# One core of a post-norm decoder layer: new orders for the attention bodies, both LayerNorms applied by ScalarE in the next body

## What is computed

```python
def _layernorm(x, eps=1e-05):
    m = mean(x); v = var(x)
    return (x - m) / sqrt(v + eps)

def attn(x):          # 3 heads of width 512; the softmax runs over the query axis (axis=2)
    Q, K, V = einsum('bne,hde->hbnd', x, Wq), ..., ...
    w = softmax(einsum('hbnd,hbmd->hbnm', Q, K) / sqrt(512), axis=2)
    return mean(einsum('hbnm,hbmd->hbnd', w, V), axis=0) @ fc_w.T + fc_b

def xattn(q, latent): # 16 heads of width 32, keys and values from a 128-wide context, causal
    ...
    return softmax(where(causal, qh @ kh.T / sqrt(32), min)) @ vh @ Wout.T

def ffn(x):           # 64 experts, top 6 of a softmax router, capacity 128, plus one shared expert
    ...

x = _layernorm(x + attn(x))
x = _layernorm(x + xattn(x, ctx_512))
x = _layernorm(x + ffn(x))
```

## Time and profile before

| | before |
|---|---|
| median of 3 runs | 2343.31 us (2339.98 to 2346.21) |
| the profiled execution | 2345.75 us, span 2344.0 us |
| busy share of the span | TensorE 88%, VectorE 75%, ScalarE 42%, GpSimd 33% |
| one turn of the loop | 82.0 us, 14 turns |

### The profile page before, as it was taken

How to read it: one execution, slowest core, us unless ns; L and a number is a source line. 1 busy time by engine, 2 the same in 40 slices (tenths; PEclk the granted TensorE clock), 3 DMA queues, 4 the chain that set the end, 5 groups by cost and what they waited for, 6 DMA issues and landing times. The chain is left out here.

```text
span 2344.0 us, 50221 instructions
## 1 busy us (share of the span) xinstructions
PE 2062.7 (88%) x17648; PEld 1307.3 (56%) x17648; DVE 1759.2 (75%) x3790; ACT 980.6 (42%) x1515; POOL 772.8 (33%) x631
## 2 busy tenths in 40 slices
PE   7989899899889989989998953699999999999960
PEld 3556565566556556655655632466666666666640
DVE  5458888888788888878888877467777677776758
ACT  4324443443344344334433423355455554555533
POOL 1002412431342243134124314344444444454420
PEclk9999999999999999999999975799999999999985
DMA  6821001001100100110010041578788887877846
GB/s 215 110 110 40 11 29 38 18 20 38 38 9 29 38 19 19 38 38 9 29 38 12 17 142 52 149 238 247 228 251 238 244 247 229 250 238 245 247 131 243
DMA packets 132885, 268.71 MB, mean 115 GB/s; under 512 B 32304, under 2 KB 42544, under 8 KB 132848
## 3 DMA queue, kind: packets, MB, share of 16 engines
q1 hardware_dynamic: 108176, 226.13, 30.2%
q0 software_dynamic: 20480, 33.71, 7.2%
q10 hardware_dynamic: 4192, 8.39, 0.9%
HBM read 217.12 MB, written 51.12 MB: 114 GB/s over the span
## 5 line engine op out<-in xcount | busy, mean ns | idle before, releaser
L677 POOL TENSOR_SCALAR_AFFINE_SELECT x_plus_shared<-x_plus_shared 128x1024 f32<-128x1024 f32 x64 | 82.6, 1291 | 840.3 <-ACT x_plus_shared L889 840.1
L702 PE MATMUL ring<-xT_split,tion_then_expert_weights 128*128 128x256 f16 x2304 | 269.0, 274 | 7.5 <-POOL xT_split L655 3.8
L702 PE MATMUL ring<-tion_then_expert_weights,xT_split 128*128 128x512 f16 x1152 | 273.4, 390 | 1.4 <-issue 1.3
L873 ACT ACTIVATE x_plus_shared<-ring 128x512 f16<-128x512 f32 x224 | 130.2, 595 | 341.9 <-PE ring L702 309.0
L107 POOL DMA_INDIRECT slot_table<-table_records,slot_of_choice x192 | 228.3, 1189 | 86.0 <-issue 54.9
L702 PEld LDWEIGHTS ring<-xT_split,tion_then_expert_weights 128*128 128x128 f16 x2304 | 221.5, 98 | 45.0 <-issue 16.3
L702 PEld LDWEIGHTS ring<-tion_then_expert_weights,xT_split 128*128 128x128 f16 x1152 | 112.7, 100 | 138.8 <-issue 18.9
L991 DVE CUSTOM_DVE_ANT_0 quad<-quad,causal_penalty 128x128 f32<-128x128 f32 (+1 forms) x512 | 164.7, 394 | 30.7 <-PE quad L772 28.5
L1232 POOL DMA_INDIRECT expert_sums<-tion_then_expert_weights,scatter_index x64 | 151.4, 2365 | 59.0 <-POOL scatter_index L1229 55.7
L1007 DVE RECIPROCAL inv_denominator<-ring 128x256 f32<-128x256 f32 x64 | 111.9, 1749 | 68.7 <-PE ring L702 58.1
L953 DVE SCALAR_TENSOR_TENSOR x_plus_shared<-ring,x_plus_shared 128x512 f16<-128x512 f32 x192 | 130.3, 685 | 26.9 <-ACT x_plus_shared L873 26.3
(11 more groups left out here) (198 smaller groups left out, 4195.8 us busy)
## 6 DMA issues: line engine op xcount, KB each, us to landing
tion_then_expert_weights<-in_w_gate SPq DMA_DIRECT2D x64, 704.0 KB
tion_then_expert_weights<-in_w_up SPq DMA_DIRECT2D x64, 704.0 KB
tion_then_expert_weights<-in_w_down SPq DMA_DIRECT2D x64, 512.0 KB, 3.9
tion_then_expert_weights<-in_w_down SPq DMA_DIRECT2D x64, 192.0 KB, 4.0
xT_in<-in_xT SPq DMA_DIRECT2D x16, 512.0 KB, 4.4
x_in<-in_x SPq DMA_DIRECT2D x16, 512.0 KB, 3.4
expert_sums<-zero_rows SPq DMA_DIRECT2D x16, 512.0 KB, 12.9
x_rows<-x_plus_shared SPq DMA_DIRECT2D x16, 512.0 KB, 2.8
```

The costliest lines, as they stand in the source:

```text
L677: pool.affine_select(out=p32[:, g % 2, :, 0:2 * P], in_=p32[:, g % 2, :, 0:2 * P], compare_op=ALU.is_ge, fill=0.0, base=0, pattern=[[0, 4] ...
L702: last = pe.matmul(out_, left(a, c), right(b, c), start=(n == 0), stop=(n == 3 * chunks - 1))
L873: act.activation(half(0), src, ACT.Copy, scale=scale).then_inc(high, 1)
```

## The change

1. New orders of the steps for all four engines. In `PE_BODY` Y01 goes ahead of T, S00 and S01 ahead of M, V20 and V21 go behind S20, S21 and ST3. In `POOL_BODY` XB goes from the end to the place behind XS at the front, so that it waits for the O1 step of the body before; MASK2 goes ahead of the first group of scatters; the second and third group both stand behind MASK3, one right after the other, at the end of the list. In `DVE_BODY` AV1 goes behind the two last V steps, OUT0 ahead of O1.
2. VectorE's LN computes statistics, the inverse root and one new tile `shift` = -mean * rstd; it no longer applies the norms. The application goes to ScalarE as x * rstd + shift (ACTIVATE Identity), in the next body: NX2 (x2) behind Y00 and V00, NX1 (x1) behind TX.
3. VectorE's O0 now waits until ScalarE has done NX1 of this body, and OUT0 until NX2.

```diff
@@ -367,36 +367,37 @@
 
 
 PE_BODY = [
-    ("Y", 0, 0), ("C", 0, 0), ("V", 0, 0), ("V", 0, 1), ("TX", 0, 0), ("TX", 1, 0), ("T", 0, 0), ("T", 1, 0),
-    ("K", 0, 0), ("R", 0, 0), ("K", 1, 0), ("Q", 0, 0), ("Q", 1, 0), ("Y", 0, 1), ("M", 0, 0), ("C", 1, 0),
-    ("V", 1, 0), ("M", 1, 0), ("S", 0, 0), ("S", 0, 1), ("M", 2, 0), ("Y", 1, 0), ("M", 3, 0), ("Y", 1, 1),
-    ("V", 1, 1), ("MT", 0, 0), ("MT", 1, 0), ("S", 1, 0), ("ST", 0, 0), ("S", 1, 1), ("CT", 0, 0),
-    ("Y", 2, 0), ("ST", 1, 0), ("Y", 2, 1), ("ST", 2, 0), ("AV", 0, 0), ("V", 2, 0), ("S", 2, 0), ("S", 2, 1),
-    ("ST", 3, 0), ("AV", 1, 0), ("V", 2, 1), ("AV", 2, 0), ("O", 0, 0), ("AV", 3, 0), ("O", 1, 0),
-    ("OUT", 0, 0), ("OUT", 1, 0),
+    ("Y", 0, 0), ("C", 0, 0), ("V", 0, 0), ("V", 0, 1), ("TX", 0, 0), ("TX", 1, 0), ("Y", 0, 1), ("T", 0, 0),
+    ("T", 1, 0), ("C", 1, 0), ("K", 0, 0), ("R", 0, 0), ("Q", 0, 0), ("K", 1, 0), ("Q", 1, 0), ("S", 0, 0),
+    ("S", 0, 1), ("M", 0, 0), ("Y", 1, 0), ("M", 1, 0), ("V", 1, 0), ("M", 2, 0), ("Y", 1, 1), ("M", 3, 0),
+    ("V", 1, 1), ("MT", 0, 0), ("MT", 1, 0), ("CT", 0, 0), ("ST", 0, 0), ("S", 1, 0), ("S", 1, 1),
+    ("Y", 2, 0), ("ST", 1, 0), ("Y", 2, 1), ("ST", 2, 0), ("AV", 0, 0), ("S", 2, 0), ("S", 2, 1),
+    ("ST", 3, 0), ("V", 2, 0), ("V", 2, 1), ("AV", 1, 0), ("AV", 2, 0), ("O", 0, 0), ("AV", 3, 0),
+    ("O", 1, 0), ("OUT", 0, 0), ("OUT", 1, 0),
 ]
 ACT_BODY = [
-    ("C", 0, 0), ("V", 0, 0), ("Y", 0, 0), ("V", 0, 1), ("TX", 0, 0), ("TX", 1, 0), ("T", 0, 0), ("T", 1, 0),
-    ("K", 0, 0), ("K", 1, 0), ("Q", 0, 0), ("Q", 1, 0), ("Y", 0, 1), ("C", 1, 0), ("V", 1, 0), ("RM", 0, 0),
-    ("Y", 1, 0), ("S", 0, 0), ("S", 0, 1), ("Y", 1, 1), ("S1", 0, 0), ("V", 1, 1), ("ST", 0, 0), ("S", 1, 0),
-    ("S", 1, 1), ("P", 0, 0), ("Y", 2, 0), ("ST", 1, 0), ("S1", 1, 0), ("Y", 2, 1), ("P", 1, 0), ("ST", 2, 0),
-    ("V", 2, 0), ("P", 2, 0), ("S", 2, 0), ("S", 2, 1), ("ST", 3, 0), ("OM", 0, 0), ("S1", 2, 0), ("V", 2, 1),
-    ("P", 3, 0), ("OM", 1, 0), ("OM", 2, 0), ("OM", 3, 0),
+    ("C", 0, 0), ("Y", 0, 0), ("V", 0, 0), ("NX2", 0, 0), ("V", 0, 1), ("TX", 0, 0), ("TX", 1, 0),
+    ("NX1", 0, 0), ("Y", 0, 1), ("T", 0, 0), ("T", 1, 0), ("C", 1, 0), ("K", 0, 0), ("Q", 0, 0), ("Q", 1, 0),
+    ("K", 1, 0), ("S", 0, 0), ("Y", 1, 0), ("S", 0, 1), ("V", 1, 0), ("RM", 0, 0), ("Y", 1, 1), ("V", 1, 1),
+    ("S1", 0, 0), ("ST", 0, 0), ("P", 0, 0), ("S", 1, 0), ("S", 1, 1), ("ST", 1, 0), ("Y", 2, 0),
+    ("S1", 1, 0), ("Y", 2, 1), ("ST", 2, 0), ("P", 1, 0), ("P", 2, 0), ("S", 2, 0), ("OM", 0, 0), ("S", 2, 1),
+    ("S1", 2, 0), ("V", 2, 0), ("ST", 3, 0), ("V", 2, 1), ("P", 3, 0), ("OM", 1, 0), ("OM", 2, 0),
+    ("OM", 3, 0),
 ]
 DVE_BODY = [
-    ("Y", 0, 0), ("C", 0, 0), ("V", 0, 0), ("V", 0, 1), ("TX", 0, 0), ("TX", 1, 0), ("T", 0, 0), ("T", 1, 0),
-    ("K", 0, 0), ("R", 0, 0), ("K", 1, 0), ("RC", 0, 0), ("Q", 0, 0), ("Q", 1, 0), ("M", 0, 0), ("Y", 0, 1),
-    ("C", 1, 0), ("M", 1, 0), ("V", 1, 0), ("M", 2, 0), ("S", 0, 0), ("S", 0, 1), ("Y", 1, 0), ("S1", 0, 0),
-    ("M", 3, 0), ("Y", 1, 1), ("S2", 0, 0), ("MT", 0, 0), ("MT", 1, 0), ("V", 1, 1), ("RM", 0, 0),
-    ("S", 1, 0), ("S", 1, 1), ("CT", 0, 0), ("S1", 1, 0), ("RS", 0, 0), ("P", 0, 0), ("Y", 2, 0),
-    ("S2", 1, 0), ("Y", 2, 1), ("AV", 0, 0), ("P", 1, 0), ("V", 2, 0), ("S", 2, 0), ("S", 2, 1), ("P", 2, 0),
-    ("S1", 2, 0), ("AV", 1, 0), ("S2", 2, 0), ("V", 2, 1), ("OM", 0, 0), ("P", 3, 0), ("AV", 2, 0),
-    ("OM", 1, 0), ("AV", 3, 0), ("OM", 2, 0), ("OM", 3, 0), ("O", 0, 0), ("O", 1, 0), ("OUT", 0, 0),
+    ("C", 0, 0), ("Y", 0, 0), ("V", 0, 0), ("TX", 0, 0), ("TX", 1, 0), ("V", 0, 1), ("Y", 0, 1), ("T", 0, 0),
+    ("T", 1, 0), ("C", 1, 0), ("R", 0, 0), ("K", 0, 0), ("Q", 0, 0), ("RC", 0, 0), ("Q", 1, 0), ("K", 1, 0),
+    ("S", 0, 0), ("M", 0, 0), ("S", 0, 1), ("M", 1, 0), ("S1", 0, 0), ("Y", 1, 0), ("M", 2, 0), ("V", 1, 0),
+    ("M", 3, 0), ("Y", 1, 1), ("MT", 0, 0), ("MT", 1, 0), ("V", 1, 1), ("S2", 0, 0), ("RM", 0, 0),
+    ("S", 1, 0), ("CT", 0, 0), ("S", 1, 1), ("P", 0, 0), ("S1", 1, 0), ("RS", 0, 0), ("Y", 2, 0), ("Y", 2, 1),
+    ("S2", 1, 0), ("AV", 0, 0), ("S", 2, 0), ("S", 2, 1), ("P", 1, 0), ("S1", 2, 0), ("OM", 0, 0),
+    ("P", 2, 0), ("S2", 2, 0), ("V", 2, 0), ("V", 2, 1), ("AV", 1, 0), ("P", 3, 0), ("AV", 2, 0),
+    ("OM", 1, 0), ("AV", 3, 0), ("OM", 2, 0), ("OM", 3, 0), ("O", 0, 0), ("OUT", 0, 0), ("O", 1, 0),
     ("OUT", 1, 0), ("LN", 0, 0),
 ]
 POOL_BODY = [
-    ("XS", 0, 0), ("CS", 0, 0), ("MASK", 0, 0), ("MASK", 1, 0), ("SC", 1, 0), ("MASK", 2, 0), ("SC", 2, 0),
-    ("MASK", 3, 0), ("SC", 3, 0), ("XB", 0, 0),
+    ("XS", 0, 0), ("XB", 0, 0), ("CS", 0, 0), ("MASK", 0, 0), ("MASK", 1, 0), ("MASK", 2, 0), ("SC", 1, 0),
+    ("MASK", 3, 0), ("SC", 2, 0), ("SC", 3, 0),
 ]
 A_STEPS = {"Y", "V", "S", "S1", "S2", "O", "XS", "XB"}
 C_STEPS = {"NX2", "TX", "R", "RC", "RM", "CT", "RS", "SC"}
@@ -432,6 +433,7 @@
     stats = mem.sb("stats", [P, 2 * NB, 6], F32)
     mv = mem.sb("mean_var", [P, 2 * NB, 2], F32)
     rstd = mem.sb("rstd", [P, 2 * NB], F32)
+    shift = mem.sb("shift", [P, 2 * NB], F32)
     root_tmp = mem.sb("root_tmp", [P, 3, 2 * NB], F32)
     x1 = mem.sb("x1", [P, NB, E], F32)
     x1s = mem.sb("x1T_split", [P, 2, EC, N], F16)
@@ -499,6 +501,7 @@
     rmax, rexp = mem.sem("router_max"), mem.sem("router_exp")
     chosen_ready = mem.sem("chosen_ready")
     rec_used = mem.sem("records_used")
+    scaled = mem.sem("attention_row_scales")
     dve_step = mem.sem("dve_step")
     taken = mem.sem("waits_taken")
 
@@ -865,7 +868,20 @@
             def emit(b):
                 for s in b.act:
                     name, g, h = s
-                    if s in b.split:
+                    if name == "NX1":
+                        act.wait_ge(scaled, b.i)
+                        for t in range(NB):
+                            last = act.activation(x1[:, t, :], pre[:, t, :], ACT.Identity,
+                                                  scale=rstd[:, t:t + 1], bias=shift[:, t:t + 1])
+                        last.then_inc(ln1, 1)
+                    elif name == "NX2":
+                        act.wait_ge(scaled, b.i)
+                        act.wait_ge(x2_stored, b.n(0, 0, 16, 1))
+                        for t in range(NB):
+                            last = act.activation(x2[:, t, :], pre2[:, t, :], ACT.Identity,
+                                                  scale=rstd[:, NB + t:NB + t + 1], bias=shift[:, NB + t:NB + t + 1])
+                        last.then_inc(ln2, 1)
+                    elif s in b.split:
                         act.wait_ge(full, b.job(*s))
                         if name == "TX" and g == 0:
                             act.wait_ge(x2T_stored, b.n(0, 0, 16, 1))
@@ -921,22 +937,19 @@
                     links[0] += 1
                     dve.wait_ge(dve_step, done_before(b.i, LINKS_A, LINKS_B, LINKS_C) + b.i * LINKS_LN + (1 + links[0]))
 
-                def norm(parts):
-
-                    rows = [(at + t, pre[:, t, :], dst[:, t, :]) for at, pre, dst, _ in parts for t in range(NB)]
-                    for n, src, _ in rows:
+                def row_scales(rows):
+
+                    for n, src in rows:
                         last = dve.bn_stats(stats[:, n, :], src)
                     link(last)
                     own_wait(dve, taken)
-                    for n, _, _ in rows:
+                    for n, _ in rows:
                         last = dve.bn_aggr(mv[:, n, :], stats[:, n, :])
                     link(last)
                     n0, n1 = rows[0][0], rows[-1][0] + 1
                     inverse_root(dve, link, rstd[:, n0:n1], mv[:, n0:n1, 1], root_tmp[:, :, n0:n1])
-                    for n, src, dst in rows:
-                        last = dve.tensor_scalar(dst, src, mv[:, n, 0:1], rstd[:, n:n + 1], ALU.subtract, ALU.mult)
-                        if n % NB == NB - 1:
-                            last.then_inc(parts[(n - n0) // NB][3], 1)
+                    dve.scalar_tensor_tensor(shift[:, n0:n1], mv[:, n0:n1, 0], -1.0, rstd[:, n0:n1],
+                                             ALU.mult, ALU.mult).then_inc(scaled, 1)
 
                 for s in b.dve:
                     name, g, h = s
@@ -971,18 +984,19 @@
                         dve.wait_ge(full, b.job(*s))
                         if g == 0:
                             dve.wait_ge(xb_ready, b.n(1, 0, 0, 1))
+                            if b.b:
+                                dve.wait_ge(ln1, b.n(0, 1, 0, 1))
                         dve.scalar_tensor_tensor(pre[:, g, :], o[:, :], 1.0 / H, xb[:, g, :],
                                                  ALU.mult, ALU.add).then_inc(free, 1)
                     elif name == "LN":
-                        parts = []
+                        rows = []
                         if b.a:
                             dve.wait_ge(free, b.freed("O", 1, 0))
-                            parts.append((0, pre, x1, ln1))
```

(8 more changed lines are left out.)

## The result

| | median, us | range, runs |
|---|---|---|
| before | 2341.64 | 2337.86 to 2346.21, 4 |
| after | 2275.11 | 2274.09 to 2278.03, 4 |

The ratio is 0.9725, 95% interval 0.9708 to 0.9741. The changed kernel is 2.8% faster. The forecast was 2355, slower by 0.5%, with 2268 to 2385 as the range of 8 in 10; the measured time is that of rival B, 2275.

What follows compares the result with a forecast made beforehand. TensorE and VectorE, neither full, wait for each other in turn within a loop turn of 82.0 us. The new turn was 81.1 + 1.7 = 82.8, +11 us over 14 turns, making 2355 us; range of 8 in 10: 2268 to 2385.

Steps and rivals of the forecast that it cites:

- rival B: Behind AV3: nothing is held, GpSimd's chain bounds a turn of 76.2 to 77.1 us; time 2275, chance 0.25.
- LN: VectorE's LayerNorm application moved to ScalarE: TX's wait of 0.54 us goes, a gain of 0 to 0.6 per turn.
- M steps: TensorE's M steps, with Y01, S00 and S01 ahead: 1.5 us more waiting per turn, between 0 and 2.
- AV0's division: VectorE divides at once behind AV0, near 50.4 in place of 54.2 us; AV1's 2.53 wait and 1.7 of clock go.
- MASK3: GpSimd's step ahead of the eight scatters: ends near 59.8 us into the turn, where it ended at 62.9.
- the eight scatters: On GpSimd behind MASK3, without a break from 60.0 to 70.7 us, with 0.8 of stretch, between 0 and 1.5.
- The hold behind AV3: AV3's end, inside the scatter run, reaches VectorE 0.8 us after the run, at 71.5 not 66.5: 5.0, bounds 0 to 5.8.
- collision: VectorE's OM2 meets GpSimd's XS instead of OM1 meeting XB, before OUT0; costs 1.2 us in place of 3.45.
- the clock: TensorE behind a 6.8 us gap before OUT0: the 1.2 GHz level costs 1.7 us per turn, between 0 and 3.4.
- The landing: GpSimd waits for the last scatter to land before XS: 1.1 us, bounded by 0 and 2.
- CS: GpSimd's step behind XB, wanted by C0: done about 83.5 against 83.7 us, costing nothing, at most 0.5.
- A: The forecast itself: the hold moves from AV0 to AV3, -1.0 to +3.0 us per turn, 2330 to 2385; chance 0.57.

Runs made afterwards that it cites:

- e4: Changed kernel's four orders, with both LayerNorms still applied by VectorE as before the change; ratio to before 0.9724, turn 77.05 us.
- e6: Kernel before without the twelve scatters of each body; one run, only the turn is read: 78.33 us.
- e7: Changed kernel without the twelve scatters of each body; one run, only the turn is read: 74.00 us.
- e11: Kernel before with each scatter replaced by a GpSimd selection of about its length, each waited for; one run, turn 80.67 us.
- e14: e13 with GpSimd waiting for the landing after each fourth scatter; ratio to before 0.9861, turn 78.47 us.
- e15: e13 with GpSimd waiting for the landing after every scatter; ratio to before 0.9938, turn 78.42 us.
- e17: Kernel before, orders and places unchanged, with GpSimd waiting for the landing after each four scatters; ratio 1.0047, turn 80.96 us.
- e18: e8 with GpSimd waiting for the landing after each four scatters; ratio to before 0.9944, turn 79.39 us.
- e19: The changed kernel measured once more beside the kernel before; 2278.65 against 2354.82 us, ratio 0.9673, turn 77.08 us.
- e1: Kernel before with only MASK2 moved ahead of the first four scatters and MASK3 ahead of the last eight; ratio 1.0173, turn 84.35 us.
- e13: Kernel before with the twelve scatters moved into GpSimd's idle stretch of the next body; ratio 1.0250, turn 85.30 us.
- e12: Changed kernel with the scatters moved into the next body, behind XS, CS and XB; ratio to before 0.9608, turn 73.95 us.
- e16: e12 with the twelve scatters ahead of XB on GpSimd; ratio to before 0.9625, turn 73.89 us.
- e10: Changed kernel with MASK3 ahead of all twelve scatters, which then run in one row; ratio to before 1.0314, turn 86.76 us.
- e8: Changed kernel with CS ahead of XB at the front of GpSimd's body; ratio to before 0.9664, turn 75.82 us.

## Why the prediction was wrong

The unit, the two causes and most steps held. Times from Y00's first matmul, 668.00 in the shown turn, with the forecast in brackets:

- LN. TX's wait went, as predicted. e4 shows that this is worth nothing once GpSimd bounds the turn.
- M steps: 0.4 more, not 1.5. AV0 started at 48.8 (48.6), with the 0.83 of waiting for CS in it. The forecast's own parts, 48.1 - 0.54 + 1.5, give 49.1 and not 48.6, a slip of 0.5.
- AV0's division at 50.2 (50.4), no wait at AV1, no slow clock, no wait at O0 (0.4). MASK3 ends at 60.3 (59.8), the eight scatters at 71.3 (70.7), one of them stretched by 0.87 (0.8).
- **The hold behind AV3, the step that failed.** I took 5.0 us of VectorE's time, from 66.5 to 71.5, 0.8 us behind the end of the run. VectorE was free at 66.5 and divided at 67.25, in the middle of the run: it lost 0.75. OUT0 started at 70.5, not 75.9.
- Two further terms hung on it. OM2 and OM3 were done at 70.4, before XS began at 73.2: no collision (1.2). TensorE's largest gap was 1.15, and the clock stayed at 1.00 (1.7). The turn was 82.8 - 76.5 = 6.3 shorter than forecast: 5.4 for OUT0 and 1.7 for the clock, less 0.65 of waiting at Y00 and 0.15 for OUT itself.
- The landing took 1.94, not 1.1, within its bounds. CS was 0.83 late where I had taken nothing and at most 0.5.

The one long turn comes nearest to the forecast: VectorE idled 3.57 us behind AV3, OUT0 waited 3.97, and the granted clock was 0.68 over OUT0 and OUT1 (970.75 to 976.09). So what A expected of all turns happened, in part, in one of 13:

```profile
967.48 1.76 DVE L1021 RECIPROCAL inv_denominator<-ring 128x256 f32<-128x256 f32 x1 [3.57 <-PE ring L705]
...
970.75 7.03 PE L705 MATMUL ring<-wout_split,x_plus_shared 128*128 128x512 f16 x24 [3.97 <-issue]
```

So the time was B's, and partly by B's mechanism: GpSimd's chain with XS and CS as releasers. B's premise, that nothing is held behind AV3, was not what happened, and that the times agree to 1 us is in part luck: B had 76.2 to 77.1 us a turn and took the upper one, the turn was 76.5, and the difference went into 4 us outside the loop and into the distance of the profiled executions from their medians.

The error was to make a rule of 14 cases. They were one place in one order, repeated by a loop: the same step, the same 0.6 us into the same four scatters. They carried no information on how a hold depends on the place. Even they didn't bear out "0.9 us after the last scatter", which was read from one turn: of the 13 cases from 300 us on the division starts 0.8 to 0.9 us behind the end of the fourth scatter in 8, 0.1 to 0.2 behind it in 4, and once, at 999.35, 0.6 before it. The row, the only one at another place, spoke for B, and so its 0.25 was too little.

What the runs put in the rule's place: no hold was seen without the indirect DMAs (e6, e7), and none where GpSimd waited behind each instruction or behind each four (e11, e14, e15, e17, e18). How long it lasts is not a property of the run's end: behind AV3 1.8 to 4.7 us in after and 1.9 to 6.25 in the same kernel in e19, 2.8 in e1's shown turn, 4.2 to 7.25 in e13; 4.57 of idling in before. Nor is it one of AV steps alone: in e13 it also took O1 or OUT1, while in e12 and e16 products ended beside twelve scatters and none was held, which agrees with the earlier trace rows. In e17 it went although up to AV0's end GpSimd had done just the same as without the landing wait. That points to what is queued behind the scatters, not to what runs; it wasn't tested further. What decides whether an end is held, and for how long, stays open.

The Trainium skill (SBUF — State Buffer, "SBUF: two separate sides") has TensorE waiting for no one at SBUF. The rows of e1 and e10, in which TensorE halts up to 1.2 us inside AV steps beside scatters, speak against taking from it, as B's case did, that scatters hold nothing; whether SBUF is the place of it, no run here tells.

## What to carry to other kernels

A stall that repeats in every turn of a loop is one observation; before its rule is applied to a new place, look for a row in which the place differs. Parts of a reordering don't add: the GpSimd order alone cost 1.7%, the norms alone 1.2%, XB alone gained 1.0%, all the orders together 2.8%. The GpSimd order by itself moved AV steps into the scatters, and the norms by themselves made TX wait for ScalarE; the other orders took both losses away. Indirect DMAs that nobody waits for can go to the stretch where their engine is idle: that took 1.9 us from e8's turn (75.82 to 73.95), and e16, with AV3 just ahead of them, was as fast. But the same move cost the kernel before 2.5% (e13), where AV3, O1 or OUT1 was held beside them; a landing wait behind each four took it back (e14). So after such a move look in the trace at what ends beside the DMAs, in every turn and not in one: in the changed kernel AV3 was held 4.7 us in one turn and 1.9 in the others.

## What the runs showed of the hardware

- A burst of indirect DMAs on GpSimd (12 of 0.97 us, one each 1.28 us) made TensorE halt within steps of many small matmuls, by 0.3 to 1.2 us at a time (e10: 65 us in 112 cases), and delayed VectorE's sight of TensorE's ends by up to 7.25 us behind AV3 (e13). Products of 128x512 were not exempt: VectorE idled up to 6.2 us for O1 and 6.4 for OUT1 (e13). Beside the same burst nothing was held in e12 and e16. The difference isn't explained.
- The delay varied at one and the same place: 1.8 to 2.0 us in 12 turns and 4.70 in one (after), 1.9 to 2.6 and once 6.25 (e19).
- A wait for the landing behind each four, some 1.95 us where the last scatter wasn't stretched, prevented this wherever it was tried (e14, e17, e18).
- The clock of TensorE stood at 0.51 in 6.2 us of O0 behind a gap of 2.83 (e6), and at 0.71 in the 8 us from 725 on behind the gap of 6.53 in e13 (OUT0 and OUT1, 7.59 us in place of 5.34). Behind gaps of 1.15 and less in the changed kernel it stayed at 1.00. In between it went both ways in the kernel before: 0.51 behind the gap of 2.53 before AV1, 1.00 over OUT0 and OUT1 behind the gap of 2.61 (778.42 to 783.76), 0.50 behind one of 4.30 (1024.05 to 1029.40).
